# Block transposes on VectorE inside a triangular inverse, with the norm factors and the output scale regrouped, in a gated delta-rule layer

## The reference

```python
mixed = silu(causal_conv(x @ w_qkv, conv_w))          # 4 taps; q, k: 16 heads of 128, v: 32 heads
beta = sigmoid(x @ w_b);  g = -exp(A_log) * softplus(x @ w_a + dt_bias)
q = l2norm(q) * 128 ** -0.5;  k = l2norm(k)           # x * rsqrt(sum(x * x) + 1e-6)
for t in range(512):                                  # per batch and v head; state is 128 x 128
    state = state * exp(g_t)
    delta = (v_t - k_t @ state) * b_t
    state = state + outer(k_t, delta)
    o_t = q_t @ state
o = o * silu(x @ w_z);  o = o * rsqrt(mean(o * o) + 1e-6) * gamma
x = layernorm(x + o @ w_out)
x = layernorm(x + moe(rmsnorm(x)))                    # 8 experts, top 2, and a shared one
```

## Time and profile before

| | us |
|---|---|
| median of 3 runs | 2554.12 (2553.75 to 2554.24) |
| the profiled execution, its own time | 2555.36 |
| its span in the trace | 2553.6 |
| PE busy | 2409.7 (94%) |
| DVE busy | 2017.6 (79%) |
| ACT busy | 1479.5 (58%) |
| POOL busy | 1264.3 (50%) |

### The profile page before, as it was taken

The page is one execution under the profiler, slowest core; times in us unless marked ns, Lnnn a source line. Parts: engine busy times, 40 slices in busy tenths (PEclk is TensorE's granted clock), DMA queues, the critical chain, the costliest instruction groups (busy, mean ns, idle before and its releaser), DMA issues.

```text
span 2553.6 us, 57047 instructions
## 1 busy us (share of the span) xinstructions
PE 2409.7 (94%) x21614; PEld 1873.3 (73%) x21614; DVE 2017.6 (79%) x3771; ACT 1479.5 (58%) x4315; POOL 1264.3 (50%) x876
## 2 busy tenths in 40 slices
PE   5899999999999999999999999999999999997998
PEld 4677777777777777777777777777777777775665
DVE  4788888888888888888888888888888888884655
ACT  3566666666666666666566665666656666662110
POOL 3355655556555555455564545555455555552000
PEclk9999999999999999999999999999999999998999
DMA  4011010111110100101010101001011100001000
GB/s 136 26 43 34 34 51 26 43 34 51 34 43 26 51 35 34 43 26 51 34 51 26 44 33 50 35 26 50 27 51 34 45 32 26 34 13 61 25 9 17
DMA packets 32112, 98.67 MB, mean 39 GB/s; under 512 B 4320, under 2 KB 9824, under 8 KB 31584
## 3 DMA queue, kind: packets, MB, share of 16 engines
q1 hardware_dynamic: 31840, 95.02, 10.7%
HBM read 92.39 MB, written 2.62 MB: 37 GB/s over the span
## 4 chain that ended last, share of the span: by engine, by line
PE 51%; DVE 32%; issue 10%; ACT 4%; POOL 2%; DVEq 1%; POOLq 0%; DMA 0%; SPq 0%; ACTq 0%
DVE conv L1091 10%; PE bank L858 10%; PE bank L834 9%; DVE decb L1119 6%; DVE XT L1140 5%; PE bank L480 4%; PE bank L884 4%; DVE m32T L1125 3%; PE bank L933 3%; PE bank L892 3%; PE bank L898 3%; ACT og L1060 3%; DVE TT L1157 3%; PE bank L960 3%; PE bank L943 2%
## 5 line engine op out<-in xcount | busy, mean ns | idle before, releaser
L1091 DVE SCALAR_TENSOR_TENSOR conv<-bank,cw_all,conv 128x511 f32<-128x511 f32 (+2 forms) x768 | 561.9, 738 | 11.9 <-ACT conv L998 7.2
L834 PE MATMUL bank<-xT,w_kh 128*128 128x512 f32 x1024 | 540.5, 628 | 2.7 <-ACT kraw L1025 1.8
L752 POOL TENSOR_TENSOR decb<-tri_sb,bfac 128x1024 f32<-128x1024 f32 x64 | 121.4, 1897 | 850.3 <-DVE kfac L1108 809.6
L1147 DVE TENSOR_TENSOR N<-bank,lev 128x512 f16<-128x512 f32 x384 | 265.5, 691 | 297.4 <-PE bank L884 297.4
L1045 ACT ACTIVATE X<-bank 128x512 f16<-128x512 f32 x384 | 233.5, 608 | 199.7 <-PE bank L892 194.3
L858 PE MATMUL bank<-w_kh,xT 128*128 128x256 f32 x1024 | 285.2, 401 | 0.0
L975 PE MATMUL bank<-wo,ogT 128*128 128x256 f32 x1024 | 253.8, 381 | 0.0
L1048 ACT ACTIVATE XT<-bank 128x512 f16<-128x512 f32 x384 | 234.2, 610 | 0.0
L834 PEld LDWEIGHTS bank<-xT,w_kh 128*128 128x128 f32 x1024 | 160.1, 191 | 80.2 <-ACT sqj L1019 47.1
L1053 ACT ACTIVATE U<-bank 128x256 f32<-128x256 f32 x256 | 101.3, 396 | 202.6 <-PE bank L933 202.6
L975 PEld LDWEIGHTS bank<-wo,ogT 128*128 128x128 f32 x1024 | 185.9, 191 | 20.2
(11 more groups left out here) (161 smaller groups left out, 5892.2 us busy)
## 6 DMA issues: line engine op xcount, KB each, us to landing
egb<-rows SPq DMA_DIRECT2D x64, 512.0 KB, 3.6
ecb<-rows SPq DMA_DIRECT2D x64, 512.0 KB, 3.6
w_kh<-w_heads SPq DMA_DIRECT2D x16, 768.0 KB, 4.4
wo_raw<-w_out SPq DMA_DIRECT2D x16, 256.0 KB, 4.6
xT<-x_cols SPq DMA_DIRECT2D x4, 512.0 KB, 6.4
qT<-x_rows SPq DMA_DIRECT2D x4, 512.0 KB, 3.7
xT<-gate_up SPq DMA_DIRECT2D x1, 2048.0 KB, 8.2
out<-og SPq DMA_DIRECT2D x4, 512.0 KB, 2.9
```

The costliest lines, as they stand in the source:

```text
L834: mm = pe.matmul(PB[j % 2][:, :], w[:, k, g * P:(g + 1) * P], xT[:, k, b * SEQ:(b + 1) * SEQ], start=(k == 0), stop=(k == KT - 1))
L1091: dve.scalar_tensor_tensor(conv[:, g, m:], PB[j % 2][:, 0:SEQ - m], cw_all[:, head, g * TAPS + 3 - m:g * TAPS + 4 - m], conv[:, g, m:], op ...
L1147: dve.tensor_tensor(blocks(N[:, i], i, 0), packed(IB[1 - i % 2], i), blocks(lev[:, 1 + i:2 + i, :], i, 0).broadcast_to(shape), ALU.mult).t ...
```

## The change

Four things change together.

1. The inverse. `start` and `x0` on ACT are gone. A new `x0` on DVE transposes the 32x32 blocks of all of `XT` into `X` in one instruction, which is the transpose of the whole as long as only small diagonal blocks are filled. `growt` of levels 0 and 1 is gone; a step `turned` on DVE transposes the 32x32 blocks of `X` into `XT` instead. Levels 2 to 5 keep `growt`. `pairs` moves to POOL, as two masking instructions.
2. The norm factors. `norms` on DVE and `nk` become one step `kn` on POOL, with one power over 8 values for both exponents.
3. The output scale. q is no longer normalised: the 1e-6 under the output's root is scaled by q's sum of squares instead. So `qnorm`, `rqs` and `zscale` go, a small `eq` on POOL comes, and `factor` becomes an addition inside POOL's `pow`; the division by 128 moves into ACT's square.
4. Signs are moved about (beta, the level masks, `u`, `res`), at no more instructions than one at the start, and the four lists of `ORDER` are written anew. The list of ACT has `silu` 2 and 3 and `vals` one round later.

```diff
@@ ORDER (the four lists are written anew; two rows of them)
-        ("x0", 0, 1), ("u", 1, 0), ("zs", 0, 1), ("growx", 0, 1), ("growt", 0, 1), ("growx", 1, 1), ("tap", 0, 2),
+        ("u", 1, 0), ("silu", 2, 1), ("silu", 3, 1), ("vals", 0, 1), ("vals", 1, 1), ("growx", 0, 1), ("zs", 0, 1),
@@ GpSimd
-                if name == "nk":
-                    pool.wait_ge(s_ss, 2 * n + 1)
-                    pool.tensor_tensor(nk[:, p], ss[:, p, 0], expo[:, 1:2].broadcast_to([P, CH]), ALU.pow).then_inc(s_nk, 1)
-                elif name == "rqs":
-                    pool.wait_ge(s_ssq, n + 1)
-                    pool.tensor_tensor(rqs[:, p], ss[:, p, 1], expo[:, 0:1].broadcast_to([P, CH]), ALU.pow).then_inc(s_rqs, 1)
+                if name == "kn":
...
+                    pool.wait_ge(s_sq, 8 * n + 4)
...
+                    pool.tensor_scalar(ss[:, p], ssum[:, p, 0], 1e-6, None, ALU.add).then_inc(s_ssk, 1)
...
+                    pool.tensor_tensor(nr[:, p], ss[:, p].unsqueeze(1).broadcast_to([P, 2, CH]),
+                                       expk[:, :].unsqueeze(2).broadcast_to([P, 2, CH]), ALU.pow).then_inc(s_nk, 1)
+                    pool.wait_ge(s_nk, n + 1)
...
+                    for dst, what, done in ((bfac, Q_BETA, s_bfac), (kfac, Q_KEYS, s_kfac)):
+                        pool.tensor_tensor(by_chunk(dst[:, p]), by_chunk(scal(n, what, 0, CELLS)),
+                                           nr[:, p, 1].unsqueeze(2).broadcast_to([P, CH, VH]), ALU.mult).then_inc(done, 1)
+                elif name == "eq":
+                    pool.wait_ge(s_sq, 8 * n + 8)
...
+                    pool.tensor_scalar(epsq[:, n % 4], ssum[:, p, 1], P * 1e-6, P * 1e-12, ALU.mult, ALU.add).then_inc(s_epsq, 1)
-                elif name == "zscale":
...
-                    pool.tensor_tensor(zs[:, p], zs[:, p], rqs[:, p].unsqueeze(2).broadcast_to([P, CH, VH * P]),
-                                       ALU.mult).then_inc(s_zq, 1)
+                elif name == "pairs":
+                    pool.wait_ge(s_mhi, 2 * n + 2)
+                    if n > 0:
+                        pool.wait_ge(s_new, 2 * n)
+                    pool.affine_select(out=XT[:, :, :].rearrange("p x (b j) -> p x b j", j=2),
+                                       in_=mhiT[:, :, :].rearrange("p x (b j) -> p x b j", j=2), compare_op=ALU.is_equal, fill=0.0,
+                                       base=0, pattern=[[0, CELLS], [-2, P // 2], [0, 2]], channel_multiplier=1).then_inc(s_near, 1)
+                    odd = XT[:, :, :].rearrange("p x (b j) -> p x b j", j=2)[:, :, :, 1]
+                    pool.wait_ge(s_near, n + 1)
+                    pool.affine_select(out=odd, in_=odd, compare_op=ALU.not_equal, fill=1.0,
+                                       base=-1, pattern=[[0, CELLS], [-2, P // 2]], channel_multiplier=1).then_inc(s_pair, 1)
                 elif name == "pow":
...
+                    pool.tensor_tensor(by_chunk(ms[:, 1, :]), by_chunk(ms[:, 0, :]),
+                                       epsq[:, n % 4].unsqueeze(2).broadcast_to([P, CH, VH]), ALU.add).then_inc(s_mse, 1)
@@ TensorE
-                elif name == "start":
-                    pe.wait_ge(s_pair, n * 2 + 2)
-                    i0h = I0[:, :].bitcast(F16)
-                    for x in range(CELLS):
-                        mm = pe.transpose(i0h[:, x * P:(x + 1) * P], XT[:, x, :], identh[:, :])
-                    mm.then_inc(s_xp, 1)
                 elif name == "growx":
                     pe.wait_ge(s_n, 6 * n + i + 1)
-                    if i > 0:
-                        pe.wait_ge(s_xt, 6 * n + i)
+                    if 0 < i <= TURNED:
+                        pe.wait_ge(s_xv, TURNED * n + i)
+                    if i > TURNED:
+                        pe.wait_ge(s_xt, MATMUL_LEVELS * n + i - TURNED)
@@ ScalarE
-                elif name == "x0":
-                    act.wait_ge(s_xp, n + 1)
-                    act.activation(X[:, :, :], I0[:, :].bitcast(F16).rearrange("p (x n) -> p x n", x=CELLS), ACT.Copy).then_inc(s_x0, 1)
@@ VectorE
-                elif name == "norms":
...
-                elif name == "qnorm":
...
-                elif name == "pairs":
...
-                    dve.tensor_tensor(half(XT, i), half(mhiT, i), lev[:, 0, :].unsqueeze(1).broadcast_to([P, 4, P]),
-                                      ALU.mult).then_inc(s_pair, 1)
+                elif name == "x0":
+                    dve.wait_ge(s_pair, n + 1)
+                    if n > 0:
+                        dve.wait_ge(s_resp, 2 * n)
+                    dve.transpose(flat(X), flat(XT)).then_inc(s_x0, 1)
+                elif name == "turned":
+                    dve.wait_ge(s_x, 6 * n + i + 1)
+                    dve.transpose(flat(XT), flat(X)).then_inc(s_xv, 1)
-                elif name == "factor":
...
-                    dve.tensor_scalar(ms[:, 1, :], ms[:, 0, :], 1.0 / P, 1e-6, ALU.mult, ALU.add).then_inc(s_mse, 1)
```

More of the change, by code:

```diff
@@ L26 @@
 Q_BETA, Q_EG, Q_KEYS, Q_EEND = range(NQ)
+TURNED = 2
 COLS_OF = (1, 0, 2, 3)
@@ L30 @@
     "tensor": [
[L31 to L40, removed]
@@ L41 @@
-        ("start", 0, 2),
+        ("read", 2, 0), ("growx", 0, 1), ("gate", 1, 1), ("gate", 2, 1), ("join", 1, 1), ("gate", 3, 1),
+        ("growx", 1, 1), ("proj", 0, 2), ("proj", 1, 2), ("join", 2, 1), ("solve", 2, 0), ("proj", 2, 2),
+        ("growx", 2, 1), ("growt", 2, 1), ("proj", 3, 2), ("join", 3, 1), ("write", 2, 0), ("out", 0, 0),
+        ("growx", 3, 1), ("ktp", 0, 2), ("read", 3, 0), ("growt", 3, 1), ("join", 4, 1), ("out", 1, 0),
+        ("growx", 4, 1), ("solve", 3, 0), ("growt", 4, 1), ("out", 2, 0), ("join", 5, 1), ("out", 3, 0),
@@ new lines @@
+        ("growx", 5, 1), ("growt", 5, 1), ("proj", 4, 2), ("newton", 0, 1), ("ktp", 1, 2), ("proj", 5, 2),
+        ("newton", 1, 1), ("finish", 0, 1), ("proj", 6, 2), ("finish", 1, 1), ("proj", 7, 2), ("solve", 0, 1),
+        ("products", 0, 2), ("write", 0, 1), ("products", 1, 2), ("turn", 0, 0), ("read", 1, 1), ("turn", 1, 0),
+        ("project", 0, 0), ("project", 1, 0), ("solve", 1, 1), ("project", 2, 0), ("project", 3, 0), ("vtp", 0, 2),
+        ("write", 1, 1), ("vtp", 1, 2), ("join", 0, 2), ("gate", 0, 2),
@@ L49 @@
-        ("turn", 1, 0), ("silu", 3, 2), ("vals", 0, 2), ("vals", 1, 2),
+        ("u", 1, 0), ("silu", 2, 1), ("silu", 3, 1), ("vals", 0, 1), ("vals", 1, 1), ("growx", 0, 1), ("zs", 0, 1),
+        ("growx", 1, 1), ("zs", 1, 1), ("tap", 0, 2), ("u", 2, 0), ("growx", 2, 1), ("growt", 2, 1), ("silu", 0, 2),
+        ("tap", 1, 2), ("growx", 3, 1), ("squares", 0, 2), ("growt", 3, 1), ("kraw", 0, 2), ("u", 3, 0),
+        ("growx", 4, 1), ("growt", 4, 1), ("power", 0, 0), ("growx", 5, 1), ("silu", 1, 2), ("growt", 5, 1),
@@ L50 @@
+        ("squares", 1, 2), ("tap", 2, 2), ("power", 1, 0), ("u", 0, 1), ("tap", 3, 2), ("turn", 0, 0), ("turn", 1, 0),
     ],
     "vector": [
[L52 to L55, removed]
@@ L56 @@
[L56 to L58 removed]
+        ("join", 2, 1), ("conv", 0, 2), ("conv", 1, 2), ("conv", 2, 2), ("join", 3, 1), ("s", 2, 0), ("conv", 3, 2),
+        ("join", 4, 1), ("rhs", 3, 0), ("og", 0, 0), ("conv", 4, 2), ("conv", 5, 2), ("join", 5, 1), ("scan", 0, 2),
@@ L59 @@
+        ("scan", 1, 2), ("res", 0, 1), ("og", 1, 0), ("res", 1, 1), ("tt", 0, 1), ("tt", 1, 1), ("conv", 6, 2),
+        ("conv", 7, 2), ("conv", 8, 2), ("s", 0, 1), ("conv", 9, 2), ("m", 0, 2), ("m", 1, 2), ("rhs", 1, 1),
+        ("conv", 10, 2), ("conv", 11, 2), ("p", 0, 2), ("p", 1, 2), ("x0", 0, 2), ("acc", 0, 0), ("s", 1, 1),
+        ("join", 0, 2), ("rhs", 2, 1), ("turned", 0, 2), ("join", 1, 2), ("acc", 1, 0), ("turned", 1, 2),
     ],
     "pool": [
-        ("rqs", 0, 0), ("mlo", 0, 1), ("zscale", 0, 0), ("diag", 0, 2), ("keys", 0, 2), ("pow", 0, 0), ("ogs", 0, 0),
@@ L62 @@
-        ("ogs", 1, 0), ("nk", 0, 2), ("mhi", 0, 2), ("mhi", 1, 2), ("qe", 0, 2),
+        ("eq", 0, 1), ("mlo", 0, 1), ("qe", 0, 1), ("keys", 0, 1), ("kn", 0, 2), ("diag", 0, 2), ("pow", 0, 0),
+        ("ogs", 0, 0), ("ogs", 1, 0), ("mhi", 0, 2), ("mhi", 1, 2), ("pairs", 0, 2),
     ],
```

102 lines of the change are left out of this document (50 added, 52 removed).

## The result

The changed kernel takes 2603.05 us (2602.67 to 2604.27), the kernel before 2554.18 us: the ratio is 1.0192, with a 95% interval of 1.0174 to 1.0209. It is slower by 49 us, where 58 us less were forecast.

The account below looks back on a forecast made before the run. PE, busy 33.96 of 35.33 us a round, was taken as the bound. Work -0.94, wait at `start` -0.87, new waits +0.5, +0.2, +0.2: together -0.9 us a round, -58 us for 64, so 2496 us; range 2470 to 2530.

Parts of the forecast that it names:

- The step that failed: On POOL: the masks of `pairs` cost 1.10 and 0.66 us, covered by DVE's work, so the move costs nothing.
- The clock: PE's granted clock, nine tenths or more in every slice but one, takes nothing that a change could give back.
- The new waits: On PE per round: 0.5 us at `x0`, 0.2 at `finish`, 0.2 at `growx` of level 4.
- PE's part: One `start` (0.46 us) and two `growt` (0.24 us each) leave PE: 0.94 us per body, 60 us over 64.
- The transposes' price: Three 128x1024 transposes on DVE cost 1.22 us each, 3.7 us together; bounds 0.82 and 2.42 us.
- The level chain: From `growx` 0 to `growx` 1 through ACT's copy, `turned` and masked copy: 2.96 us, covered by PE's 3.24 us.
- The transposes stand behind POOL: POOL's work holds DVE's three transposes by 0.8 us each: +0.9 us a round, 2612 us; chance 0.10.
- The transposes take the gain back: DVE's transposes at 1.8 us each outrun the level chains' covers and delay `x0`: 2573 us; chance 0.12.
- The waits go too: `x0`, `finish` and level 4 cost PE nothing: 1.81 us less a round, 2438 us; chance 0.15.
- The change doesn't do what it says: The new order of the four queues loses as much elsewhere as is won: 2554 us; chance 0.05.
- `kn`: On POOL, `kn` takes 2.8 us ahead of `diag`; the scans come about 0.35 us later after the squares.
- that sign of a wrong forecast: Scans waiting for POOL's `decb` would put `kn` on the path and make the forecast wrong from POOL's side.

Follow-up runs that it names:

- e1: The changed kernel with the first mask of the start split into two masks over every second column: 2370.16 us, ratio to before 0.9282.
- e2: The changed kernel with both masks of the start replaced by one product on POOL with the level mask: 2367.66 us, ratio to before 0.9270.
- e3: The changed kernel with two unused fp32 products of 128x512 added on PE ahead of the first `join`: 2545.36 us, ratio to before 0.9964.
- e5: e1 with `growt` of levels 0 and 1 on PE and ACT again, instead of DVE's `turned`: 2399.36 us, ratio to before 0.9396.
- e6: e2 with `start` on PE and its copy on ACT again, one part of `gate` moved ahead of the first `join`: 2466.36 us, ratio to before 0.9657.
- e8: e2 with the mask of the remainder `mloT` written over rows of two elements: 2366.53 us, ratio to before 0.9271.
- e10: e2 with level 2's transposed half also made by DVE's block transpose (`TURNED = 3`): 2425.54 us, ratio to before 0.9498.
- e7: e2 with the mask's product on POOL made twice, one behind the other: 2479.86 us, ratio to before 0.9709.
- e4: The changed kernel with the mask as one product on DVE directly ahead of `x0`: 2394.69 us, ratio to before 0.9374.

## Why the prediction was wrong

- **The step that failed** is the price of `pairs` on POOL: "`pairs` costs 1.10 us as the masking of `mloT` does, and 0.66 us". It was made by the number of values, and the diff showed a loop over two values inside. The two took 4.49 and 0.76 us, with gaps 5.5 us from the end of `mhi` (1214.44) to `x0`, instead of 1.76. So "The move of `pairs` costs nothing, and the wait for POOL's mask is covered too" fell with it: PE waited 2.44 us at `x0`, where 0.5 was forecast. e1 and e2 show it, since nothing but the mask was changed there.
- **The clock** was set aside as something a change here could not move, because it was high before. It moved downward, by 58 us (e3). A wait that is new can cost more than its length.
- **The new waits** of 0.9 us in the sum (`x0` 0.5, `finish` 0.2, level 4 0.2) do not exist once the mask is short: e2's windows show no idle time of PE. A round lost 2.97 us against before, not 0.9: the 0.94 us of work, all of the 1.37 us of idle time, and 0.66 us that the trace of before counted as busy. So the ceiling that the prediction set, PE's own work and 1.37 us, was too low as well: it took the busy time of the trace, which has modelled ends of matmuls, as work. Before, PE's weight loads of `proj` waited for ACT's `squares` while PE counted as busy (us in total, times, longest):

```profile
PEld bank L834 <- ACT sqj L1019: 8.4, 12, 0.7
```

That is 8.4 us of 400, and in e2 these waits are gone. Whether such waits make up the 0.66 us was not tested. The lower end of the range, 2445 us, would have missed the repaired kernel.
- **PE's part** held: 0.48 us for two `growt` was measured as 29 us (e5), 31 by the sum. By the 390 ns per transpose on TensorE that the Trainium skill gives in "VectorE: DVE Perf Modes", section "The three transpose paths", `start` alone would have made e6 some 200 us slower, an estimate (8 x 0.39 x 64). It was 99 us slower, waits included.
- **The transposes' price** held: 1.22 us expected, 1.245 measured, and the longest of all 192 is 1.248 us. The level chain held too: from `growx` 0 to `growx` 1 1226.16 - 1222.91 = 3.25 us with no idle time between, for 3.24 us of cover.
- **The rivals.** "The transposes stand behind POOL" gave 2612 us, near the measured time, but for the wrong reason: none of the 192 transposes was held. POOL ran `mlo` beside every `x0` and `qE` beside every first `turned`; the second `turned` started only as `keys` ended, so in the changed kernel not all three fell into POOL's 7 us, as the rival had it. In e8 all three did, and took 1.25 us at most. The Trainium skill says in "SBUF — State Buffer", section "Who interferes with whom", that an instruction with one SBUF input isn't held unless it runs in a mode with both ports; if it counts the transpose so, the trace agrees. "The transposes take the gain back" is false for levels 0 and 1 (e5) and true for level 2's half in the place that e10 gave it. "The waits go too", 0.15, has the direction of the change without its mask, but its 2438 us are 70 us above e2. "The change doesn't do what it says" is out: with the same lists e2 is 187 us faster than before.
- **`kn`** took 2.38 us from its first instruction to `diag`, for 2.8 in the sum, since POOL's small instructions cost 0.20 to 0.23 us. The scans wait 0.7 us for `decb` each round, in e2 as well, where PE has no idle time. So that sign of a wrong forecast was no cause.

Waits up to 1.94 us left the clock alone (e7). Left open is why the same wait of 2.44 us lowered the clock in one round and not in the next.

## What to carry to other kernels

Price an instruction by its loops as well as by its values, above all where a rearranged view has a short inner dimension, and try the same mask as a product, or column by column. When a step moves to an engine that has idle time, what matters is whether something waits for it: some 3 us more on POOL cost 235 us ahead of `x0` (e2 against the changed kernel, 58 us of them by the clock), and 3.4 us more cost nothing behind it (e8). Where PE nearly never stands, look at what a new wait does to its granted clock before adding up the waits themselves.

## What the hardware showed that I had not expected

- A mask on POOL over 1024 fp16 values takes 1.09 us in rows of 128 and 4.48 us in rows of two (e8).
- A wait of 2.44 us on PE was followed in half of the rounds by more than 3 us at half clock, for 1.6 us more per round, and a wait of 2.98 us in twelve of 15; waits of 1.40 and 1.94 us never were (e7).
- Eight cells masked on DVE by one product took 0.76 us in three rounds of four, and 1.30 us in the fourth, when more of it lay beside POOL's `mlo` (e4).
- A transpose of 32x32 blocks on DVE, 128x1024 in fp16, took 1.25 us at most beside POOL's reading (e8).
